# Cross attention with unscaled probabilities, outputs multiplied by spread reciprocals, norms on Pool, and the last norm and the routing inside the MoE stage

## What is computed

```python
# q = x, k = v = context; the residual is k, the context
x = layernorm(x + mamba(x))                      # its last steps run inside the cross attention stage
attn = softmax(where(mask, -inf, (q @ w_q) @ (k @ w_k).T / 8))          # 16 heads of 64
out = (attn @ (v @ w_v)) @ w_o + b_o
y = (out + k - mean) / (std + 1e-3) * gamma + beta
x = layernorm(x + y)
x = layernorm(x + shared_expert(x) + routed_experts(x, top2(softmax(x @ router_w))))
```

## Time and profile before

| | us |
|---|---|
| three runs | 2800.72, 2802.37, 2805.56 |
| median | 2802.37 |
| the profiled execution, its own time | 2800.31 |
| its span, first to last instruction | 2798.5 |
| PE busy in it | 2495.3 (89%) |
| DVE busy | 1757.8 (63%) |
| ACT busy | 1353.4 (48%) |
| POOL busy | 1151.2 (41%) |

### The profile page before, as it was taken

The page is one execution under the profiler, slowest core; times in us unless marked ns, Lnnn a source line. Parts: engine busy times, 40 slices in busy tenths (PEclk is TensorE's granted clock), DMA queues, the critical chain, the costliest instruction groups (busy, mean ns, idle before and its releaser), DMA issues. The chain is left out here.

```text
span 2798.5 us, 47512 instructions
## 1 busy us (share of the span) xinstructions
PE 2495.3 (89%) x18594; PEld 1497.2 (54%) x18594; DVE 1757.8 (63%) x3458; ACT 1353.4 (48%) x2380; POOL 1151.2 (41%) x612
## 2 busy tenths in 40 slices
PE   5999989999997778999998799999989898788899
PEld 2334434344343334544444588999845455566557
DVE  3899889989999657777767630111335667466433
ACT  4566665665664246666665321111256766222231
POOL 2788889889889613333333201222110000200030
PEclk8999999999999999999999899999989999999999
DMA  5031130321212153343334153555220000200020
GB/s 217 1 128 61 60 136 2 120 88 49 121 51 116 28 156 70 81 100 81 85 78 115 32 189 133 182 177 186 87 74 1 1 1 2 91 9 1 1 107 31
DMA packets 126094, 227.22 MB, mean 81 GB/s; under 512 B 7888, under 2 KB 97488, under 8 KB 109744
## 3 DMA queue, kind: packets, MB, share of 16 engines
q1 hardware_dynamic: 122128, 213.95, 23.5%
q0 software_dynamic: 3744, 10.23, 1.0%
HBM read 201.74 MB, written 22.41 MB: 80 GB/s over the span
## 5 line engine op out<-in xcount | busy, mean ns | idle before, releaser
L208 POOL TENSOR_TENSOR m_h<-m_h,m_bc 128x1024 f32<-128x1024 f32 x256 | 612.3, 2411 | 81.1 <-DVE m_h L521 81.1
L521 DVE TENSOR_TENSOR_SCAN m_h<-m_da,m_h 128x1024 f32<-128x1024 f32 x256 | 578.7, 2278 | 39.8 <-ACT m_da L411 39.8
L281 PE MATMUL m_psy<-m_h,m_ident 128*128 128x512 f32 x1024 | 494.0, 615 | 23.2 <-POOL m_h L208 23.2
L411 ACT ACTIVATE m_da<-x_rows,m_a_neg 128x511 f32<-128x511 f32 x512 | 330.7, 680 | 157.7 <-DVE m_h L521 154.4
L941 POOL TENSOR_SCALAR c_pr<-c_pr,c_share 128x512 f32<-128x512 f32 x128 | 200.4, 1565 | 391.2 <-DVE c_share L1239 391.2
L281 PEld LDWEIGHTS m_psy<-m_h,m_ident 128*128 128x128 f32 x1024 | 196.3, 196 | 288.4 <-issue 233.7
L508 DVE TENSOR_TENSOR m_h<-m_dtx,m_bc 128x1024 f32<-128x1024 f32 x192 | 232.3, 1210 | 28.8 <-PE m_psy L281 22.8
L1001 PEld LDWEIGHTS c_psO<-c_pT,c_vr 32*64 32x64 f32 x8192 | 131.0, 137 | 133.3 <-issue 130.5
L1001 PE MATMUL c_psO<-c_pT,c_vr 32*64 32x128 f32 x8192 | 162.8, 289 | 33.4 <-ACT c_oT L1132 28.8
L227 PE MATMUL m_rot<-early_ctx,early_w 128*128 128x512 f32 x240 | 126.6, 653 | 71.0 <-ACT m_gz L387 52.1
L1119 ACT ACTIVATE c_pr<-c_pr,c_low 128x512 f32<-128x512 f32 x256 | 180.9, 707 | 2.9 <-DVE c_low L1231 2.7
(11 more groups left out here) (378 smaller groups left out, 4051.0 us busy)
## 6 DMA issues: line engine op xcount, KB each, us to landing
m_bc<-bc_dram SPq DMA_DIRECT2D x32, 2048.0 KB, 7.5
e_up<-in_up SPq DMA_DIRECT2D x39, 1024.0 KB
c_vr<-v_dram SPq DMA_DIRECT2D x128, 256.0 KB
v_dram<-c_stage SPq DMA_DIRECT2D x32, 256.0 KB, 2.1
e_down<-in_down SPq DMA_DIRECT2D x8, 1024.0 KB
e_down<-y_dram SPq DMA_DIRECT2D x8, 512.0 KB, 7.4
h_w<-in_w SPq DMA_DIRECT2D x2, 2048.0 KB, 14.4
m_taps<-in_taps SPq DMA_DIRECT2D x1, 2560.0 KB, 12.2
```

Of the source, the lines that this page charges most:

```text
L208: pool.tensor_tensor(hq, hq, bc[:, 1, NP * s:NP * (s + 1), :], ALU.mult).then_inc(p_ready, 1)
L281: mm = pe.matmul(bank, ident[:], h[:, n % HB, e, :], start=False, stop=(s == NG - 1 and e == NP - 1))
L411: ins = act.activation(da[:, n % 2, e, at:at + L - 1], dt[:, u, j, at:at + L - 1], ACT.Exp, scale=a_neg[:, u, j, NP * s + e:NP * s + e + 1])
L521: dve.tensor_tensor_scan(flat, decay, flat, 0.0, ALU.mult, ALU.add).then_inc(scanned, 1)
```

## The change

- The probabilities are no longer scaled. ScalarE's and Pool's scalings go, and VectorE transposes the exponentials as soon as they are there. `share`, the reciprocals, has nine slots in place of three.
- Once per pack, in front of the scores in unit n = 4p + 8, TensorE spreads the reciprocals over psX (`turn_share`): for each tile of queries and each head a matmul whose weight is the reciprocal's column repeated 64 times and whose moving operand is the identity. VectorE then multiplies the pack's output oT by psX (`share_out`). The next extra and the output projections wait for that (`o_shared`).
- Norms: VectorE keeps statistics and reciprocals. Pool does subtraction and scaling by the norm, scale, shift and addition to x, with the batch's `before` and `behind` parts in a fixed order. The first batch's parts stay on VectorE.
- The norm of the last batch, the last turn and the whole routing product move from the end of cross attention into MoE. They run there with the first shared chunks; `res`, the rows with gamma and beta, and the statistics are carried over. The new order on TensorE is lift 0, route 0 to 11, lower 0, turn_last, lift 1, route 12 to 15, lower 1, lift 2, count, lower 2, lift 3, lift 4, seat, lower 3, lift 5, lower 4, lower 5. The store of x's rows for the gather is split in two, the second part behind the norm.

```diff
-                def scale(n):
-                    pool.wait_ge(share_ready, n + 1)
-                    s = pr[:, n % 3, 0, :]
-                    pool.tensor_scalar(s, s, share[:, n % 3, 0:1], None, ALU.mult).then_inc(p_scaled[0], 1)
-
-                for n in range(TOTAL):
-                    scale(n)
-                    if n % UNITS == 24:
-                        pool.wait_ge(res_loaded, 16 * (n // UNITS) + 16)
-                        pool.wait_ge(loaded[2], 32)
-                        pool.tensor_tensor(res[:], res[:], rows[:, 0:1, :].broadcast_to([P, LT, D]), ALU.add)\
-                            .then_inc(res_ready, 1)
+                steps = [0]
+
+                def link(ins):
+                    steps[0] += 1
+                    ins.then_inc(pool_step, 1)
+                    pool.wait_ge(pool_step, steps[0])
+
+                batch = lambda b: x[:, LT * b:LT * (b + 1), :]
+                wide = lambda a: a.broadcast_to([P, LT, D])
+
+                def apply(rows, mean, inverse):
+                    for t in range(LT):
+                        ins = pool.tensor_scalar(rows[:, t, :], rows[:, t, :], mean[:, t, 0:1], inverse[:, t:t + 1],
+                                                 ALU.subtract, ALU.mult)
+                        if t == LT - 1:
+                            return ins
+                        ins.then_inc(pool_step, 1)
+                        steps[0] += 1
+
+                def before(b):
+                    pool.wait_ge(n_ready, norm_no["yo", b] + 1)
+                    link(apply(yo, n_mv, n_std))
+                    link(pool.tensor_tensor(yo[:], yo[:], wide(gb[:, 0:1, :]), ALU.mult))
+                    link(pool.tensor_tensor(yo[:], yo[:], wide(gb[:, 1:2, :]), ALU.add))
+                    pool.wait_ge(x_loaded[1], 16 * (NB - 1))
+                    link(pool.tensor_tensor(batch(b), batch(b), yo[:], ALU.add))
+                    pool.nop().then_inc(yo_added, 1)
+                    pool.wait_ge(n_ready, norm_no["x", b] + 1)
+                    link(apply(batch(b), n_mv, n_std))
+                    pool.nop().then_inc(before_ready, 1)
+
+                def behind(b):
+                    pool.wait_ge(r_ready, b + 1)
+                    link(apply(res, mv, std))
+                    link(pool.tensor_tensor(res[:], res[:], wide(rows[:, 1:2, :]), ALU.mult))
+                    link(pool.tensor_tensor(res[:], res[:], wide(rows[:, 2:3, :]), ALU.add))
+                    link(pool.tensor_tensor(batch(b), batch(b), res[:], ALU.add))
+                    pool.nop().then_inc(added, 1)
+                    pool.wait_ge(n_ready, norm_no["next", b] + 1)
+                    link(apply(batch(b), n_mv, n_std))
+                    pool.nop().then_inc(behind_ready, 1)
+
+                for b in range(NB):
+                    if b + 1 < NB:
+                        before(b + 1)
+                    if b >= 1:
+                        behind(b - 1)
+                    pool.wait_ge(res_loaded, 16 * b + 16)
+                    pool.wait_ge(loaded[2], 32)
+                    pool.tensor_tensor(res[:], res[:], wide(rows[:, 0:1, :]), ALU.add).then_inc(res_ready, 1)
 
             @block.tensor
...
 
+                def turn_share(p):
+                    n = LT * p + 2 * LT
+                    pe.wait_ge(x_free, sum(k < n for k in numbers))
+                    if p >= 1:
+                        pe.wait_ge(o_shared, p)
+                    pe.wait_ge(share_ready, LT * (p + 1))
+                    for t in range(LT):
+                        for i in range(2):
+                            mm = pe.matmul(psX[HD * i:HD * (i + 1), t * P:(t + 1) * P],
+                                           share[:, (LT * p + t) % 9, i:i + 1].broadcast_to([P, HD]), ident[:], start=True, stop=True)
+                    mm.then_inc(share_full, 1)
+
...
+                    if n >= 2 * LT:
+                        pe.wait_ge(o_shared, n // LT - 1)
                     if b + 1 < NB and u in BEFORE:
...
-                for n in range(TOTAL + 8):
+                for n in range(TOTAL + 2 * LT):
                     b, u = divmod(n, UNITS)
+                    if n >= 2 * LT and n % LT == 0:
+                        turn_share(n // LT - 2)
                     if n + 2 < TOTAL:
                         needed(n + 2)
                         scores(n + 2)
...
-                def scale(n):
-                    act.wait_ge(share_ready, n + 1)
-                    s = pr[:, n % 3, 1, :]
-                    act.activation(s, s, ACT.Copy, scale=share[:, n % 3, 1:2]).then_inc(p_scaled[1], 1)
...
                 def turn(n):
                     p, t = divmod(n, LT)
                     if p >= 2:
                         dve.wait_ge(attended, p - 1)
                     for i in range(2):
-                        dve.wait_ge(p_scaled[i], n + 1)
+                        dve.wait_ge(p_ready, 2 * n + i + 1)
                         dve.transpose(pT[:, p % 2, i, t, :], pr[:, n % 3, i, :]).then_inc(turned, 1)
+
+                def share_out(p):
+                    dve.wait_ge(o_kept, p + 1)
+                    dve.wait_ge(share_full, p + 1)
+                    dve.tensor_tensor(oT[:, p % NM, :], oT[:, p % NM, :], psX[:], ALU.mult).then_inc(o_shared, 1)
...
-                    xs = x[:, LT * b:LT * (b + 1), :]
-                    link(dve.tensor_tensor(xs, xs, res[:], ALU.add))
-                    dve.nop().then_inc(added, 1)
+                    dve.reciprocal(std[:], std[:]).then_inc(r_ready, 1)
...
+                def invert_n(*use):
+                    dve.wait_ge(n_root, norm_no[use] + 1)
+                    dve.reciprocal(n_std[:], n_std[:]).then_inc(n_ready, 1)
...
                 def x_stats(b):
+                    dve.wait_ge(yo_added, b + 1)
                     norm_stats(batch(b), "x", b)
 
...
                 def next_stats(b):
+                    dve.wait_ge(before_ready, min(b + 3, NB))
+                    dve.wait_ge(added, b + 1)
                     norm_stats(batch(b), "next", b)
...
-                before_parts = {0: yo_stats, 2: yo_apply, 3: yo_scale, 4: yo_shift, 5: yo_add, 6: x_stats, 9: x_apply}
-                behind_parts = {19: next_stats, 23: next_apply}
-                norm_parts = {8: statistics, 11: normalise, 13: scale, 15: shift, 17: add_to_x}
-
-                for part in before_parts.values():
+                first_parts = [yo_stats, yo_apply, yo_scale, yo_shift, yo_add, x_stats, x_apply]
+                before_parts = {0: yo_stats, 2: lambda b: invert_n("yo", b), 6: x_stats, 8: lambda b: invert_n("x", b)}
+                behind_parts = {16: next_stats, 18: lambda b: invert_n("next", b)}
+                norm_parts = {8: statistics, 10: invert_std}
+
...
+                    if n >= 2 * LT and n % LT == 0:
+                        share_out(n // LT - 2)
...
+                by_tile = rows_dram.rearrange("(t p) c -> p t c", p=P)
+                sp.dma_start(by_tile[:, 0:NT - LT, :], x[:, 0:NT - LT, :]).then_inc(kept[0], 16)
                 for e in range(NR):
                     if e == HELD:
+                        sp.wait_ge(last_ready, 1)
+                        sp.dma_start(by_tile[:, NT - LT:NT, :], x[:, NT - LT:NT, :]).then_inc(kept[1], 16)
                         sp.wait_ge(seats_full, 1)
                     sp.dma_start(down[:, e], d["down"][1 + e]).then_inc(w_loaded, 16)
...
+
+                def turn_last():
+                    pe.wait_ge(last_ready, 1)
+                    for k in range(KD):
+                        for t in range(LT):
+                            mm = pe.transpose(psE[:, 2 * k, t * P:(t + 1) * P], x[:, NT - LT + t, k * P:(k + 1) * P], ident[:])
+                        mm.then_inc(last_turned, 1)
+
                 pe.wait_ge(ahead.shared_loaded, 32)
                 lift(0)
+                pe.wait_ge(loaded, 80)
+                for t in range(NT - LT):
+                    route(t)
+                lower(0)
+                turn_last()
                 lift(1)
+                pe.wait_ge(last_kept, KD)
+                for t in range(NT - LT, NT):
+                    mm = route(t)
+                mm.then_inc(logits, 1)
+                lower(1)
+                lift(2)
                 count()
-                lower(0)
-                lift(2)
-                lower(1)
+                lower(2)
                 lift(3)
+                lift(4)
                 seat()
-                lower(2)
-                lift(4)
                 lower(3)
...
+                act.wait_ge(last_var, 1)
+                act.activation(rstd[:, 0], mv[:, 0, :, 1], ACT.Sqrt, scale=D / (D - 1)).then_inc(last_root, 1)
+                shared(0)
+                act.wait_ge(last_var, 2)
+                act.wait_ge(eps_ready, 1)
+                act.activation(rstd[:, 1], mv[:, 1, :, 1], ACT.Sqrt, bias=eps[:]).then_inc(last_root, 1)
+                for k in range(KD):
+                    act.wait_ge(last_turned, k + 1)
```

(20 more changed lines are left out.)

150 lines of the change are left out of this document (66 added, 84 removed).

## The result

The changed kernel takes 2817.6 us (median of 6 runs, 2812.6 to 2822.0) against 2805.0 for the kernel before (6 runs, 2800.7 to 2810.2): a ratio of 1.0039, 95% interval 1.0028 to 1.0050. It is slower by 0.39%, some 11 us (12.6 between the medians), inside the range and on the side that had most of the chance, where the point had said +2.6 against the earlier median (+5 by the sum). Its profiled execution took 2822.0, 4.4 above its median (span 2820.2, against 2798.5 before).

A forecast was written before the change was run, and what follows sets the result against it. TensorE was taken to bound units with a projection, output or turn, VectorE plain units. Cross attention +12 and the move into MoE -7 gave +5: span 2803.5, time 2805 us, range 2791 to 2821.

The forecast's parts named there:

- the edge: Between cross attention and MoE: 10.9 us of routing and turn replace an edge of 17.9, a gain of 7.0.
- D: turn_share's 16 matmul records on TensorE, once per pack: 1.4 us from a four-tile profile row, bounds 0.95 and 1.8.
- halves at once: Rival: turn_share's two column halves overlap wholly, 0.95 us per pack, 11 less in all, time 2794; chance 0.2.
- The copy wait: In front of turn_share, TensorE waits for ScalarE's copy of psX: 0.74 us per TensorE-bound pack.
- Packs behind a turn: Packs following a turn of x: four cost 1.0 us more each for busy ScalarE; unit 12 of batch 0 costs 2.9.
- What is added in all: Cost of turn_share and share_out, 32 times in cross attention, with waits and tail: 63.0 us.
- What comes back: Cross attention time regained by freeing VectorE and ScalarE: 51 of 64.9 us, bounds 35 and 57.
- the excess of 64.9: Time of the four cross attention batches over their 478.2 us floor by kind of unit, from norms, table loads and scaling.
- Small waits, 2.4: Small waits in batches 1 to 3, 2.4 us of the 14 expected to stay over the floor.
- freed engines were not the excess: Rival: only 35 us come back in cross attention, +16, time 2821; chance 0.1.
- The yo chain: Norm work Pool takes over: 10.9 us against 10.5 available in batch 0, hence about 1 us late there.
- The tail: End of cross attention, two turn_shares in line: +1.1 less 0.5, and +1.7, together 2.3 us.

The follow-up runs named there:

- second profiles: The kernel before and the changed kernel, unchanged, each profiled once more: spans 2803.4 and 2814.8 us, executions 2805.2 and 2816.6 us.
- experiment 3: Changed kernel without turn_share, share_out and their waits, outputs left undivided by the softmax sums: 2761.0 us, ratio 0.9837.
- Experiment 4: Changed kernel with turn_share moved behind the scores of its unit and share_out behind the row maximum: 2793.4 us, ratio 0.9953.
- experiment 1: Kernel before with only the move of routing, last norm and last turn into MoE: 2803.6 us, ratio 0.9992.
- experiment 6: Changed kernel with routing and last norm put back at the end of cross attention, that norm on VectorE: 2819.0 us, ratio 1.0044.
- experiment 11: Changed kernel with V's loads asked for one unit later and nothing else: 2807.1 us, ratio 1.0000.
- experiment 12: Kernel before with V's loads asked for one unit later and nothing else: 2806.3 us, ratio 0.9998.
- experiment 5: Kernel of Experiment 4 with the 2 MB of shared weights asked for at unit 21 of batch 3 instead of unit 15: 2792.1 us, ratio 0.9955.
- experiment 9: Kernel of Experiment 4 with V's loads asked for one unit later: 2787.7 us, ratio 0.9942.

## Why the prediction was right or wrong

The sign and the range held. The sum was +12 for cross attention and -7 for the edge; measured by the second profiles it is +19.0 (+12.2 in the loop, +6.8 in the tail) and -6.4. The mechanism was right and several terms were mis-sized. That the sum came as near as it did is partly luck: by experiment 3 the added part was put 9 us too high and the part that comes back 13 too high, and one error hid most of the other.

*D.* Put at 1.4, the four-tile row, it measured 1.02, near the lower bound of 0.95. The row that was taken as nearest was not: two tiles of 64 columns overlap almost wholly. The rule of the Trainium skill, TensorE: Matmul & The Clock Gate, Part 3, that matmuls in distinct column groups run at once, gives 0.95 here, an estimate (8 x 0.117), and agrees with this trace within 0.07 us. The rival "halves at once" was thus true in its condition and false in its time (2794), since it left all other terms as they were.

*The copy wait.* 0.74 was predicted and 0.76 measured from the same point, 1.78 for the pack with D instead of 2.15. Experiment 4 shows that this wait and most of the cost behind a turn were avoidable: they go when the scores stand ahead.

*Packs behind a turn.* Put at 15.5 for five, measured 21.2 (3.9, 5.5, 5.1, 2.9 and 3.9). The wait itself was right: 0.74 + 1.0 predicted, 1.79 to 1.85 measured from the same point in all five, with or without table loads before it. Of the rest 1.7 belongs to the table loads of two packs and is there without the spreading too (3.62 for a floor of 2.79). With the measured D and wait five packs are 14.2, so some 5.3 are left. The step that failed is that TensorE was taken to run at full speed behind the wait, where the rows show it at the lower clock: the 16 records take 1.14 to 1.91 instead of 1.02.

*What is added in all.* The prediction said 63.0; experiment 3 gives 57 by the medians and 54.3 by the profiles (50.2 in the loop, 4.1 in the tail). Too much by 6 to 9, mostly for D's sake (0.38 in each of 25 packs).

*What comes back.* The prediction said 51 of the excess of 64.9; experiment 3 gives 38.2, as 26.7 stay where 14 were left. This is the term that failed, by 13. "Small waits, 2.4" had no room for TensorE's "issue" stalls, which in that kernel are 8.3 us in the loop and 12.5 with the tail. Nor had it one for TensorE's clock in the plain units of batch 0 behind the statistics of yo: scores take 2.08 us there instead of 1.13, VectorE waits 0.33 to 0.39 for them, and three units take 3.02 each instead of 2.63. The statistics of batches 1 and 2 are hidden, as I had thought: the step that holds them takes 4.98 or 5.05 us, the next one 3.24 or 3.17, and the two together are twice the 4.11 of the floor. The rival "freed engines were not the excess" (35 come back) came near this number, and its time of 2821 was too high only because the added part was smaller.

*Pool.* A tensor_scalar with two operations takes 1.22, not 0.8 (the line's view of Pool in the changed kernel):

```profile
L950 POOL TENSOR_SCALAR c_yo<-c_yo,c_n_mv,c_spare 128x256 f32<-128x256 f32 x12 | 14.5, 1221 | 237.5 <-DVE c_spare L1316 237.5
```

Halving the one-operation price of 512 elements was too simple. The yo chain is 12.1 instead of 10.9 and is late only in batch 0, as foreseen.

*The tail.* +2.3 predicted, +6.8 measured. Of the 4.5 between them the profiles put 4.3 down to "issue" (5.9 against 1.6 us in stalls that end after the last reciprocal; part of the longest lies before it).

*The edge.* -7 predicted, -6.4 and -8.0 measured in the trace, with the routing at 5.67 and 1.85, the turn at 1.04 and no wait for it, and 21 us of cover. Two misses cancel here by luck: routing and turn took 8.1 us instead of the 10.9 put down, while lower(0) at a granted clock of 0.82 (8.58 for 7.07) and the start of the stage (2.25 for 1.02) took 2.7 more. Yet experiments 1 and 6 both price the move at 1.0 to 1.4 us of the whole, which is not clear of noise. The step that failed is not in the edge: I counted the removal of code from the end of cross attention as free for the code before it. With the move TensorE's "issue" stalls in cross attention grow by 3 (experiment 1) and by 5.7 (changed kernel against experiment 6). That they grow is shown; why the position of the fetches shifts with the program's text is argued only, as no view shows the addresses of instructions.

*The size of the loss.* With V's loads one unit later the changed kernel equals the kernel before (experiment 11), and the kernel before doesn't move (experiment 12). With that wait 8 to 9 us of stalls and 10.5 us of time go, so one wait on SyncE is worth as much as the whole loss. It is not the only such part. Moving turn_share behind the scores takes 24 us while the stalls stay at 14.1 (experiment 4), so the uncovered copy of psX is worth more than twice the loss. The loss is what is left between costs and gains of some 40 to 60 us, and no single one of them is its cause. What can be said is which of them the prediction had no term for: the growth of the "issue" stalls, 10 us by the second profiles, is larger than the 6 to 8 us by which the measured loss exceeds the predicted 5.

What these stalls are is in part argued. My first theory, the shared weights, fell in experiment 5. The Trainium skill, Runtime: NRT & Kernel Launch, Instruction fetch mechanics, states that each sequencer fetches its instructions through a DMA queue of its own in blocks of 16 KiB, the next page while the current one runs, and that this is mostly hidden. The packets of 16 KB agree; "mostly hidden" does not fit 14.3 to 15.1 us of stalls in cross attention, if they are fetches. That the fetch itself queues behind V's small rows rests on the order of packets at the three long stalls and on the two interventions (9 and 11). The wait on SyncE also delays what stands behind V's loads in its list, and what in V's loads blocks the fetch, their number of packets or their bytes, stays open; it was not tried with V in larger rows.

*What was said to show.* Batch 1 was put near 152 (158.3 and 155.6), batch 2 near 152 (153.1 and 152.8), batch 3 near 118 (117.3, 117.2), batch 0 unchanged (+3.2 and +2.9), steps of 6.3 (5.89), idle 0.7 (0.69). The picture was right in the pack and in batches 2 and 3; batch 0 grew by 3, where no change was expected, and batch 1 by 4 to 6 more than was expected.

The version with the lowest median is that of experiment 9, 2787.7 us, 0.6% under the kernel before.

## What to carry to other kernels

A new matmul that writes a shared bank should stand behind work that doesn't need the bank, so that the hand-over copy is covered: moving two calls by one position was worth 24 us here, twice what the whole change cost. When an expected gain doesn't arrive, add up the stalls without a releaser before and after, and look at what the DMA queues move just before them: here a large load moved by one unit returned 10.5 us. Statistics or square roots moved by one unit need the other engines' due times read first; a cost seen in one unit may already be repaid in the next.

## What the runs showed of the hardware

- Two column halves of 64, all 128 rows, 128 moving columns: 16 records in 1.02 us, 0.064 a record, where full-array records take 0.117 and four tiles of 32 columns take 0.35 for 8.
- TensorE can stand 2.8 to 5.6 us with no wait of its own in the middle of the loop, at the same units from execution to execution (5.60 and 5.05; 3.43 and 3.43). At the long stalls a 16 KB packet of the instruction queue arrives only after V's load (four transfers of 256 KB in small rows, DMA engines 95% busy), and TensorE goes on 2 to 4 us after it.
- After a stall of 1.7 us in front of turn_share the next 16 records took 1.81 us for 1.09 and four records of scores 2.05 for 1.13, at a granted clock of 0.54, TensorE's lower level.
- On Pool a tensor_scalar with two operations and per-row scalars takes 1.22 us for 256 elements, and one with one operation 1.565 for 512.
- A part of the program that didn't change became slower by 3 us when text behind it was moved away (experiment 1; 546.2 against 543.1 and 542.9).
- Two table loads around a square root take 1.28 us each on ScalarE. TensorE waited 0.86 us for a copy behind them, and 2.76 us where they stood between the copies of two turns.
